# Two attention layers: six mask products become ScalarE copies, batch 0's feed-forward products move into the last body, head 1 comes first

## The chip, the cores and the metric

The kernel runs on one core of a Trainium2 chip. The metric is the device time of one execution in microseconds. A core has five engines with an instruction queue of their own: TensorE (PE, with its weight loads as PEld), VectorE (DVE), ScalarE (ACT), GpSimd (POOL) and SyncE (SP), which here only issues transfers.

## The reference, cut to what matters

Eight batches of 256 tokens with 128 features, fp32, go through two layers; a context of the same shape gives keys and values, with 16 heads of 8 features.

```python
x = x + xattn0(layernorm(x), ctx)          # softmax(q k / sqrt(8)) v, projection; no mask
x = x + ffn(layernorm(x))                  # the feed-forward part
x = x + xattn1(layernorm(x), ctx, mask)    # logits + mask * -1e9, 256 x 256 per batch
x = x + moe(layernorm(x))                  # 8 experts, 512 hidden, the best 2 of a token

def ffn(x):
    h = bit_linear(x, w1)                  # 128 -> 512; rows rounded to 8 bits, weights to -1, 0, 1
    h = silu(depthwise_conv1d(h, conv_w, conv_b))   # 3 taps along the tokens
    return bit_linear(h, w2)               # 512 -> 128; the rows of h rounded to 8 bits
```

## The kernel before, in words

**Order.** Every engine's queue is written out by hand. The program runs in stages: the first layer's attention (35 to 169 us in the profiled execution), its feed-forward part (to 247 us), the second layer's attention (to about 404 us), and the experts, whose tokens are gathered and scattered in DRAM. Semaphores tie the queues; a wait holds everything that stands behind it on its engine.

**Attention as a chain of bodies.** Each engine goes through bodies b = -1, 0, ..., NB (NB = 8), and in a body through the head numbers n = 0 to 15. Body b works on three batches. At head n, for batch b+1, TensorE makes the scores, queries on the partitions (`scores`, L1658), and VectorE takes their row maxima: `plain_max` (L1289) in the first layer, `masked_max` (L1303, one instruction for each half of the keys) in the second. For batch b TensorE makes the same scores again with the keys on the partitions and with the row maximum taken off (`shifted`, L1743), ScalarE takes the exponential of 128 x 512 (L1023), and after every four heads TensorE multiplies with V (`weighted_v`, L1698). For batch b-1 the body finishes: the fourth product with V, `out_transposes` (L1852), VectorE's `head_norm` (L1263, L1269), `norm_transposes` (L1860), ScalarE's copy `o_normT` (L1036), `projection` (L1867), `residual_stats` (L1282, then L428 and L434), GpSimd's `ln_power` (L439, L441), `ln_apply` (L447), and in the first layer `quant_factors` (L458 to L462) and `quantise_rows` on GpSimd. The body NB of the first layer has only finishing work; its second part ("tail") lies inside the first feed-forward steps.

**The mask.** In the second layer a shifted product has three matmuls: first a diagonal matrix times the mask of the batch, 512 columns (L1740), which sets the accumulation to -mask x 1e9, then the two score products with `start=False`.

**How the maxima get into the shifted product.** They are an additional row of the stack `q_stack`. GpSimd's `max_parts` (L817, L819) splits the maxima of eight heads, TensorE transposes them (`max_transposes`, L1635), ScalarE copies them (`maxT`, L967), and a transfer writes them into the stack. Half 0 belongs to the heads 0 to 7, half 1 to the heads 8 to 15. In `extras` the transposes of half 1 stand behind shifted product n = `at["max1"]`.

**Where a step stands.** The table `STEPS` gives for each step the head number of either layer. Keys without a prefix are TensorE's, `a_` is ScalarE's, `d_` VectorE's: `max1` and `a_max1` the transposes and the copy of half 1, `a_out1` the copy of the second half of the output, `d_ln` `ln_apply`, `d_quant` `quant_factors`. `None` means that no head has it.

**PSUM banks.** Scores use banks 0 and 1 in turn, shifted products 2, 3 and 4, the output 5 and 6, and bank 7 the rest. So score n waits for the maximum of head n-2 and a shifted product for the exponential of three heads before (`head_bank`).

**The feed-forward part.** `ffn_hidden` makes the hidden products of a batch in four chunks of 128: half 0 (chunks 0 and 1) with the three taps as three accumulated matmuls (L1674 to L1676), half 1 (chunks 2 and 3) with one matmul each, whose taps then come from ScalarE's `conv_middle` (L915, L916) and VectorE's `conv_sides` (L924, L930). Then `ffn_silu` on ScalarE, `act_transposes` on TensorE (L1954), `quant_scale` on VectorE (the scale of each row), `rounding` on ScalarE (L1155), `quant_clip` on GpSimd (L762, its output f_int), `int_transposes` (L1965), and `output` (L1974). A batch thus passes from engine to engine several times. `ternary_taps` makes the three tap matrices on GpSimd, in body NB-2.

Before the change batch 0's hidden products stand at head 2 of the body NB, behind the wait for the last exponential; batch 1's half 0 at head 8 of the same body, and batch 0's `act_transposes` and batch 1's half 1 behind the body, when the last `head_norm` is done.

Of the kernel before, what the change touches and what calls it, by code (L numbers as in the profile page):

```python
# [18 lines left out]
F32 = mybir.dt.float32  # L19
# [25 lines left out]
    "max1": (0, 2),  # L45
# [12 lines left out]
    "a_out1": (0, 0),  # L58
# [11 lines left out]
    "d_ln": (11, 12),  # L70
# [5 lines left out]
def build(nc, inp, out):  # L76
# [27 lines left out]
    with ExitStack() as ctx:  # L104
# [9 lines left out]
        BANKS_T = (2, 3, 4)  # L114
        BANK_O = (5, 6)
# [185 lines left out]
        class Att:  # L301

            def __init__(self, n):
# [15 lines left out]
                if n == "a0":  # L319
                    return  # L320
                self.k_in, self.k_q, self.k_k = s("mask_in"), s("mask_q"), s("mask_k")
# [442 lines left out]
        def attention_gpsimd(eng, l, part, between={}):  # L764
# [3 lines left out]
            def body(b, r):  # L768
# [55 lines left out]
        def _(eng):  # L824
# [74 lines left out]
            attention_gpsimd(eng, 0, "main 0", {-1: add_output_bias, 0: routing_constants, 1: ternary, NB - 2: ternary_taps})  # L899
# [10 lines left out]
        def conv_middle(eng, b, r):  # L910
# [5 lines left out]
            eng.activation(conv_out[:, r, 1, :], hidden_ps(r, 3), ACT.Copy, scale=conv_w[:, 3, 1:2]).then_inc(h_mid, 1)  # L916

# [94 lines left out]
        def attention_scalar(eng, l, part, between={}):  # L1012
# [305 lines left out]
        def attention_vector(eng, l, part, between={}):  # L1318
# [3 lines left out]
            def body(b, r):  # L1322
                for n in range(H):
# [173 lines left out]

        def ffn_vector(eng):
# [6 lines left out]

            def quant_scale(b):

                for i in range(NT):
                    eng.wait_ge(g_ps, b * NT + i + 1)
# [611 lines left out]
```

## Time and profile before

| | |
|---|---|
| median of 3 runs | 509.7 us (509.5 to 510.54) |
| the profiled execution | 508.18 us, its span 506.4 us |
| TensorE busy | 443.3 us, 88% of the span |
| VectorE busy | 345.9 us, 68% |
| ScalarE busy | 301.6 us, 60% |
| GpSimd busy | 226.5 us, 45% |
| TensorE's mean granted clock | 0.98 of full speed |

The span is from the first to the last instruction that the profiler saw; the execution's time has 1.8 us more around it. The share of an engine is an average over stages with different limits, so the rows below are mostly from single stages. "idle before" in a group of instructions is the time that the engine had nothing to do ahead of them, and the instruction named behind it is the one that ended most of that time.

### The profile page before, as it was taken

The page shows a single profiled execution, that of the slowest core. Times are in us where ns is not written, and L with a number is a line of the kernel's source. Part 1 is how long each engine was busy: PE and PEld are TensorE (multiplying, and loading weights), DVE is VectorE, ACT ScalarE, POOL GpSimd, SP SyncE. Part 2 cuts the span into 40 slices and gives each one's busy share as a digit, 9 for nine tenths or more (in the row PEclk, how much of TensorE's full clock was granted, in tenths as well). Part 3 has the DMA queues.
Part 4 walks back from the last instruction along what each step waited for, and adds up shares of the span by engine and source line. Part 5 has one row for each costly group of instructions (what it writes and reads, how often), then busy time and mean ns, then how long its engine had stood idle before and what let it go on. Part 6 is the DMA issues. An engine that isn't in the chain of part 4 may idle for free.

```text
span 506.4 us, 11481 instructions
## 1 busy us (share of the span) xinstructions
PE 443.3 (88%) x3709; PEld 363.2 (72%) x3709; DVE 345.9 (68%) x1233; ACT 301.6 (60%) x649; POOL 226.5 (45%) x455
## 2 busy tenths in 40 slices
PE   3689999999998779967999999999999889899960
PEld 2477777777775668856778878777777579899960
DVE  6767787878783267877887788787878266444424
ACT  5237776767767448874466756566556555455630
POOL 4752464123216245767200225354453566666650
PEclk9999999999999989989999999999999999999995
DMA  6463323332405995034253234333320301332107
GB/s 216 150 223 105 115 85 116 102 101 77 137 4 207 426 415 213 2 105 130 84 159 113 88 107 158 118 122 94 112 61 2 87 23 39 85 85 82 53 15 249
DMA packets 40698, 61.55 MB, mean 122 GB/s; under 512 B 6121, under 2 KB 30506, under 8 KB 39232
## 3 DMA queue, kind: packets, MB, share of 16 engines
q1 hardware_dynamic: 38080, 56.20, 34.0%
q0 software_dynamic: 2272, 4.24, 2.6%
q8 instruction: 30, 0.49, 0.4%
q10 hardware_dynamic: 288, 0.39, 0.3%
q14 instruction: 28, 0.23, 0.2%
HBM read 31.45 MB, written 29.23 MB: 120 GB/s over the span
## 4 chain that ended last, share of the span: by engine, by line
PE 45%; DVE 10%; issue 5%; ACT 4%; DMA 3%; SPq 2%; POOL 1%; POOLq 0%; DVEq 0%; ACTq 0%
PE ps L1698 6%; PE ps L1658 6%; PE ps L1740 6%; PE ps L1743 5%; PE ps L1889 5%; PE ps L1900 5%; ACT probs L1023 2%; PE ps L1867 1%; DMA k_blocks<-y_dram 1%; DVE ps L1303 1%; PE ps L1954 1%; PE ps L1674 1%; SPq L544 1%; PE ps L1675 1%; PE ps L1676 1%
## 5 line engine op out<-in xcount | busy, mean ns | idle before, releaser
L1023 ACT ACTIVATE probs<-ps 128x512 f32<-128x512 f32 x256 | 147.0, 598 | 79.6 <-PE ps L1743 75.0
L1658 PE MATMUL ps<-k_blocks,q_stacks 128*128 128x256 f32 x512 | 117.9, 314 | 6.4 <-DVE row_max L1289 3.0
L1289 DVE TENSOR_REDUCE row_max<-ps 128x2 f32<-128x512 f32 x144 | 94.9, 686 | 26.9 <-PE ps L1658 25.7
L1743 PE MATMUL ps<-q_stacks,k_blocks 128*128 128x256 f32 x512 | 104.9, 288 | 1.2 <-DMA q_stacks<-maxT 1.0
L1303 DVE CUSTOM_DVE_ANT_0 ps<-ps,mask_q 128x256 f32<-128x256 f32 x224 | 89.8, 452 | 20.6 <-PE ps L1658 18.9
L1743 PEld LDWEIGHTS ps<-q_stacks,k_blocks 128*128 128x128 f32 x512 | 86.8, 189 | 20.8 <-issue 10.6
L1658 PEld LDWEIGHTS ps<-k_blocks,q_stacks 128*128 128x128 f32 x512 | 82.6, 197 | 13.9 <-issue 4.3
L1698 PE MATMUL ps<-probs,v_aug 128*32 128x256 f32 x1024 | 68.5, 385 | 4.3 <-ACT probs L1023 3.1
L817 POOL TENSOR_SCALAR max_split<-row_max 128x16 fp32r<-128x16 f32 x32 | 6.5, 204 | 124.3 <-issue 93.0
L1740 PE MATMUL ps<-mask_k,neg_mask_eye 128*128 128x512 f32 x128 | 54.5, 426 | 0.0
L739 POOL DMA_INDIRECT y_dram<-x_ring x39 | 39.1, 1003 | 22.6 <-ACT x_ring L1102 14.2
L1698 PEld LDWEIGHTS ps<-probs,v_aug 128*32 128x32 f32 x1024 | 27.8, 109 | 24.1 <-ACT probs L1023 6.2
L1889 PE MATMUL ps<-m_xT,m_w 128*128 128x128 f32 x312 | 41.8, 277 | 2.9 <-DVE m_w L1449 1.7
L1900 PE MATMUL ps<-conv_out,m_h 128*128 128x128 f32 x312 | 41.2, 276 | 0.0
L1889 PEld LDWEIGHTS ps<-m_xT,m_w 128*128 128x128 f32 x312 | 37.9, 192 | 4.1 <-DVE m_w L1449 3.0
L1455 DVE COPY conv_out<-experts 128x512 f32 x39 | 18.3, 469 | 31.2 <-PE ps L1900 31.1
L729 POOL DMA_INDIRECT slots_dram<-rows,r_slot x32 | 32.4, 1011 | 13.8 <-issue 7.8
L1900 PEld LDWEIGHTS ps<-conv_out,m_h 128*128 128x128 f32 x312 | 37.9, 192 | 0.0
L1740 PEld LDWEIGHTS ps<-mask_k,neg_mask_eye 128*128 128x128 f32 x128 | 24.0, 188 | 12.8 <-issue 11.9
L1303 DVE DVE_READ_ACCUMULATOR2_ANT row_max<- 128x1 f32 x224 | 31.9, 142 | 0.0
L439 POOL TENSOR_SCALAR ln_ve<-ln_mv 128x2 f32<-128x2 f32 x24 | 5.8, 240 | 52.4 <-DVE ln_mv L434 52.3
L1090 ACT ACTIVATE m_xT<-ps 128x128 f32<-128x128 f32 x39 | 10.8, 277 | 25.1 <-PE ps L1880 25.1
(217 smaller groups left out, 760.1 us busy)
## 6 DMA issues: line engine op xcount, KB each, us to landing
slots_dram<-x_ring SPq DMA_DIRECT2D x1, 10400.0 KB, 30.1
q_stacks<-q_dram SPq DMA_DIRECT2D x32, 256.0 KB
k_blocks<-k_dram SPq DMA_DIRECT2D x128, 48.0 KB
q_dram<-qk_parts SPq DMA_DIRECT2D x16, 256.0 KB, 2.9
k_dram<-qk_parts SPq DMA_DIRECT2D x16, 256.0 KB, 2.9
mask_in<-host_mask SPq DMA_DIRECT2D x8, 512.0 KB, 3.6
experts<-host_experts SPq DMA_DIRECT2D x1, 4096.0 KB, 39.1
x_ring<-slots_dram SPq DMA_DIRECT2D x39, 65.0 KB
```

Source lines behind the costliest of these rows:

```text
L729: eng.indirect_dma_start(out=slots_dram[:, :], out_offset=bass.IndirectOffsetOnAxis(ap=r_slot[r][:, k, i:i + 1], axis=0), in_=rows[:, r, k ...
L739: eng.indirect_dma_start(out=y_dram[:, :], out_offset=bass.IndirectOffsetOnAxis(ap=x_ring[:, slot, D:D + 1].bitcast(U32), axis=0), in_=x_r ...
L1023: eng.activation(probs[:, n // HPS % 2, n % HPS, :, :].rearrange("p k q -> p (k q)"), ps[:, head_bank(BANKS_T, n)[0], :], ACT.Exp).then_in ...
L1289: eng.tensor_reduce(row_max[:, :, n], ps[:, head_bank(BANKS_S, n)[0], :].rearrange("p (i k) -> p i k", i=NT), AX.X, ALU.max).then_inc(a.s_ ...
L1303: last = eng.tensor_tensor_reduce(out=scored, in0=scored, in1=mask_q[t % 2][:, i, :], scale=1.0, scalar=-3.0e38, op0=ALU.add, op1=ALU.max, ...
L1455: eng.tensor_copy(m_down[:, j % 2, :, :].rearrange("p c d -> p (c d)"), experts[:, bass.ds(weight_at[j] + EH, EC * D)]).then_inc(m_weights, 1)
L1658: mm = eng.matmul(ps[:, bank, i * S:(i + 1) * S], q_stack[r][:, st, i * P:(i + 1) * P], k_blocks[r][:, st, j, :], start=not masked, stop=n ...
L1698: mm = eng.matmul(ps[j * HR:(j + 1) * HR, bank, 0:S], v_aug[r][:, k, first:first + HR], probs[:, st % 2, j, k, :], start=(odd == 0 and k = ...
L1740: eng.matmul(ps[:, bank, :], neg_mask_eye[:, :], mask_k[b % 3][:, :, :].rearrange("p i k -> p (i k)"), start=True, stop=False)
L1743: mm = eng.matmul(ps[:, bank, k * S:(k + 1) * S], k_blocks[r][:, st, j, k * P:(k + 1) * P], q_stack[r][:, st, :], start=(l == 0), stop=(l ...
L1889: mm = eng.matmul(ps[:, BANK_W[j % 2], c * P:(c + 1) * P], m_w[:, j % WR, c * P:(c + 1) * P], m_xT[:, j % 2, :], start=True, stop=True)
L1900: mm = eng.matmul(ps[:, BANK_Y[j % 2], 0:D], m_h[:, j % 2, c, :], m_down[:, j % 2, c, :], start=(c == 0), stop=(c == EC - 1))
```

## The change

The parts, by layer:

- First layer: at head 1 of each body TensorE issues score 1, shifted product 1, the transposes of the maxima of half 1 (now `second_max`) and the fourth product with V of the batch before, in this order; until now it was the transposes, score 1, that product with V, and shifted 1. ScalarE's `a_out1` goes from head 0 to head 1.
- First layer: `ln_apply` goes from VectorE to GpSimd, behind `ln_power`.
- `ternary_taps` goes from body 6 to body 3 on GpSimd.
- Batch 0's hidden products go into body 7: half 1 at head 3, chunk 0 at head 6, chunk 1 at head 8. The middle tap of its chunks 2 and 3 is made by VectorE (`first_middle`) at head 6 of that body, the side taps right behind it.
- In the body NB, batch 1's half 1 stands at head 2, its chunk 0 at head 4, and behind `norm_transposes` batch 0's `act_transposes` and batch 1's chunk 1. Batch 0's silu stands at head 2 of ScalarE's body, both halves together; one small silu at the end of body 7 brings its table. VectorE makes batch 0's `quant_scale` at head 6 of the body, and the last batch's `quant_factors` go behind the tail's start.
- Second layer: for the heads 5, 7, 8, 11, 13 and 15 (`SEEDED`) ScalarE copies the mask, times -`MASK_A`, as 128 x 512 numbers from SBUF into the PSUM bank (`mask_seed`), and TensorE leaves out the 512-column product L1740. ScalarE does so behind its exponentials 2, 4, 5, 8, 10 and 12 (`SEED_STEPS`); the copy waits for the end of the exponential that frees the bank.

```diff
@@ STEPS
-    "max1": (0, 2),
+    "max1": (None, 2),
...
-    "a_out1": (0, 0),
+    "a_out1": (1, 0),
...
-    "d_ln": (11, 12),
+    "d_ln": (None, 12),
@@ build
+        SEEDED = (5, 7, 8, 11, 13, 15)
+        SEED_STEPS = (2, 4, 5, 8, 10, 12)
@@ attention_gpsimd, body
                     ln_power(eng, s, b - 1)
+                    if l == 0:
+                        ln_apply(eng, s, b - 1)
...
-            attention_gpsimd(eng, 0, "main 0", {-1: add_output_bias, 0: routing_constants, 1: ternary, NB - 2: ternary_taps})
+            attention_gpsimd(eng, 0, "main 0", {-1: add_output_bias, 0: routing_constants, 1: ternary, 3: ternary_taps})
@@ ScalarE
+        def first_middle(eng):
+
+            eng.wait_ge(h_ps, 1)
+            for c in range(TAPPED, FC):
+                last = eng.tensor_scalar(conv_out[:, 0, c - TAPPED, :], hidden_ps(0, c), conv_w[:, c, 1:2], None, ALU.mult)
+            last.then_inc(h_mid, 1)
...
             if half == 0:
-                eng.wait_ge(h_ps, b * 2 + 1)
+                eng.wait_ge(h_ps, b * 2 + 2)
@@ attention_scalar, body
                                        ps[:, head_bank(BANKS_T, n)[0], :], ACT.Exp).then_inc(a.p_sb, 1)
+                    if l == 1 and exists(b) and n in SEED_STEPS:
+                        mask_seed(b, SEEDED[SEED_STEPS.index(n)])
...
-                    if l == 0 and isinstance(b, int) and b == NB and n == 5:
+                    if l == 0 and b == NB - 1 and n == H - 1:
+                        eng.activation(r_gap[:, :], minus_half[:, 0:NT], ACT.Silu)
+                    if l == 0 and b == NB and n == 2:
                         eng.wait_ge(a.pv, NB * 4 - 1)
-                        conv_middle(eng, 0, 0)
                         ffn_silu(eng, 0, 0, 0)
-                    if l == 0 and isinstance(b, int) and b == NB and n == 10:
                         ffn_silu(eng, 0, 0, 1)
...
+            def mask_seed(b, n):
+
+                if n == SEEDED[0]:
+                    eng.wait_ge(a.k_k, b + 1)
+                eng.wait_ge(a.p_sb, b * 16 + n - 2 if n < H - 1 else b * 16 + 12)
+                eng.activation(ps[:, head_bank(BANKS_T, n)[0], :],
+                               mask_k[b % 3][:, :, :].bitcast(F32).rearrange("p i k -> p (i k)"),
+                               ACT.Copy, scale=-MASK_A).then_inc(a.t_seed, 1)
@@ attention_vector, body
-                    if n == at["d_ln"] and exists(b - 1):
-                        if l == 0:
-                            ln_apply(eng, s, b - 1)
-                        else:
-                            ln_rows(eng, b - 1, 1 - r)
-                    if l == 0 and n == at["d_quant"] and exists(b - 1):
+                    if l == 1 and n == at["d_ln"] and exists(b - 1):
+                        ln_rows(eng, b - 1, 1 - r)
+                    if l == 0 and n == at["d_quant"] and exists(b - 1) and b < NB:
                         quant_factors(eng, s, b - 1)
-                    if l == 0 and isinstance(b, int) and b == NB and n == 6:
+                    if l == 0 and n == 0 and b == NB + 1:
+                        quant_factors(eng, s, NB - 1)
+                    if l == 0 and b == NB - 1 and n == 6:
+                        first_middle(eng)
                         conv_sides(eng, 0, 0)
+                    if l == 0 and b == NB and n == 6:
+                        quant_scale(eng, 0)
@@ ffn_vector, step (quant_scale itself is moved out of it, unchanged)
-                quant_scale(b)
+                if b > 0:
+                    quant_scale(eng, b)
@@ attention_tensor, body
+                    ahead = l == 0 and n == at["pv"] % HPS and exists(b)
+                    if ahead:
+                        shifted(b, r, n)
+                        second_max(b)
                     if n % HPS == at["pv"] % HPS:
...
-                    if exists(b):
+                    if exists(b) and not ahead:
                         shifted(b, r, n)
                     extras(b, r, n)
+
+            def second_max(b):
+
+                if after(b, 0):
+                    eng.wait_ge(a.o_sb, b * 2 - 1)
+                max_transposes(eng, l, b, 1)
@@ shifted
-                if l == 1:
+                seeded = l == 1 and n in SEEDED
+                if seeded:
+                    eng.wait_ge(a.t_seed, b * len(SEEDED) + SEEDED.index(n) + 1)
+                elif l == 1:
                     eng.matmul(ps[:, bank, :], neg_mask_eye[:, :], mask_k[b % 3][:, :, :].rearrange("p i k -> p (i k)"),
                                start=True, stop=False)
...
-                                    q_stack[r][:, st, :], start=(l == 0), stop=(l == 0 or k == NT - 1))
+                                    q_stack[r][:, st, :], start=(l == 0), stop=(l == 0 or k == NT - 1),
+                                    skip_group_check=seeded)
@@ extras (ffn_hidden takes a tuple of chunks now)
-                if l == 0 and isinstance(b, int) and b == NB and n == 2:
+                if l == 0 and b == NB - 1 and n == 3:
 
                     eng.wait_ge(a.s_max, NB * 16)
+                    eng.wait_ge(f_tern, 9)
+                    ffn_hidden(eng, 0, 0, 1)
+                if l == 0 and b == NB - 1 and n in (6, 8):
+                    ffn_hidden(eng, 0, 0, 0, (n // 2 - 3,))
+                if l == 0 and b == NB and n == 2:
                     eng.wait_ge(a.p_sb, NB * 16)
-                    eng.wait_ge(f_tern, 9)
-                    for half in range(2):
-                        ffn_hidden(eng, 0, 0, half)
-                if l == 0 and isinstance(b, int) and b == NB and n == 8:
-                    ffn_hidden(eng, 1, 1, 0)
+                    ffn_hidden(eng, 1, 1, 1)
+                if l == 0 and b == NB and n == 4:
+                    ffn_hidden(eng, 1, 1, 0, (0,))
...
                 if n == at["max1"] and exists(b):
-                    if after(b, 0):
-                        eng.wait_ge(a.o_sb, b * 2 - 1)
-                    max_transposes(eng, l, b, 1)
+                    second_max(b)
...
                         norm_transposes(eng, l, b - 1)
+                        if l == 0 and b == NB:
+                            act_transposes(eng, 0)
+                            ffn_hidden(eng, 1, 1, 0, (1,))
@@ ffn_tensor (act_transposes itself is moved out of it, unchanged)
-
-            eng.wait_ge(att[0].o_norm, NB * 2)
-            act_transposes(0)
-            ffn_hidden(eng, 1, 1, 1)
```

## Rows read from the trace of the kernel before

**Rows 1.** The page: busy us of each engine, share of the span, instructions.

```profile
PE 443.3 (88%) x3709; PEld 363.2 (72%) x3709; DVE 345.9 (68%) x1233; ACT 301.6 (60%) x649; POOL 226.5 (45%) x455
```

**Rows 2.** Windows: stretch, length, busy PE PEld DVE ACT POOL (count), granted clock, DMA, GB/s.

```profile
35.50:153.50 118.00, 111.49 (x1058) 86.69 (x1058) 94.96 (x219) 85.01 (x169) 38.24 (x80) 1.00 0.31 93
169.40:193.90 24.50, 20.40 (x114) 17.64 (x111) 12.56 (x39) 13.53 (x30) 7.18 (x13) 0.93 1.03 428
264.10:387.00 122.90, 122.31 (x1055) 96.22 (x1055) 101.18 (x511) 75.66 (x162) 48.14 (x141) 1.00 0.34 104
```

**Rows 3.** Groups by line and form: busy, mean ns of one | idle before them.

```profile
L967 ACT ACTIVATE maxT<-ps 8x512 f32<-8x512 f32 x32 | 18.5, 579 | 8.9 <-PE ps L1635 8.4
...
L1222 ACT ACTIVATE k_blocks<-o_normT 128x2048 fp32r<-128x2048 f32 x2 | 3.8, 1916 | 0.0
...
L447 POOL TENSOR_SCALAR xn<-x_res,ln_mv,ln_rstd 128x128 f32<-128x128 f32 x16 | 12.7, 798 | 0.9
...
L447 DVE TENSOR_SCALAR xn<-x_res,ln_mv,ln_rstd 128x128 f32<-128x128 f32 x16 | 4.8, 344 | 3.1 <-POOL ln_rstd L441 2.5
```

**Rows 4.** Timeline, start of body 4: start, us, instruction, count [wait before it].

```profile
101.67 0.40 PE L1743 MATMUL ps<-q_stacks,k_blocks 128*128 128x256 f32 x2
...
102.65 0.41 PE L1635 MATMUL ps<-ident_r,max_split 128*8 128x128 f32 x4 [0.58 <-POOL max_split L819]
...
104.62 0.40 PE L1658 MATMUL ps<-k_blocks,q_stacks 128*128 128x256 f32 x2
```

**Rows 5.** Timeline, end of body 4.

```profile
115.33 0.60 DVE L447 TENSOR_SCALAR xn<-x_res,ln_mv,ln_rstd 128x128 f32<-128x128 f32 x2
...
117.05 0.41 DVE L458 TENSOR_REDUCE qa<-xn 128x2 f32<-128x256 f32 x1
...
118.60 0.47 PE L1658 MATMUL ps<-k_blocks,q_stacks 128*128 128x256 f32 x2 [0.30 <-DVE row_max L1289]
```

**Rows 6.** Timeline, body 7 and the start of the feed-forward part.

```profile
157.91 1.07 PE L1698 MATMUL ps<-probs,v_aug 128*32 128x256 f32 x16 [0.48 <-ACT probs L1023]
...
160.87 0.71 PE L1867 MATMUL ps<-w_all,o_normT 128*128 128x128 f32 x4 [0.20 <-ACT o_normT L1036]
...
165.23 1.07 PE L1698 MATMUL ps<-probs,v_aug 128*32 128x256 f32 x16 [1.03 <-ACT probs L1023]
...
169.40 0.70 PE L1674 MATMUL ps<-xnT_all,w_taps 128*128 128x256 f32 x2
...
172.95 0.60 PE L1852 MATMUL ps<-ident,o_raw 128*128 128x128 f32 x4
...
177.27 0.61 PE L1867 MATMUL ps<-w_all,o_normT 128*128 128x128 f32 x4
...
186.76 1.30 POOL L762 TENSOR_SCALAR f_int<-probs 128x512 bf16<-128x512 int16 x2
...
188.59 1.06 PE L1965 MATMUL ps<-ident_bf,f_int 128*128 128x128 bf16 x8
```

**Rows 7.** Waits of TensorE's weight loads, 264 to 388 us: total us, times, longest.

```profile
PEld ps L1867 <- ACT o_normT L1036: 1.4, 6, 0.2
...
PEld ps L1658 <- DVE row_max L1303: 1.0, 4, 0.3
```

**Rows 8.** Timeline, a full body of the second layer.

```profile
331.19 0.60 PE L1852 MATMUL ps<-ident,o_raw 128*128 128x128 f32 x4
...
335.79 0.30 PEld L1658 LDWEIGHTS ps<-k_blocks,q_stacks 128*128 128x128 f32 x2 [0.26 <-DVE row_max L1303]
...
345.65 0.40 PE L1740 MATMUL ps<-mask_k,neg_mask_eye 128*128 128x512 f32 x1
345.89 0.40 PE L1743 MATMUL ps<-q_stacks,k_blocks 128*128 128x256 f32 x2
...
352.07 0.60 PE L1852 MATMUL ps<-ident,o_raw 128*128 128x128 f32 x4
```

**Rows 9.** Timeline, last body of the second layer.

```profile
401.13 1.07 PE L1698 MATMUL ps<-probs,v_aug 128*32 128x256 f32 x16 [0.38 <-ACT probs L1023]
```

More of the change, by code:

```diff
@@ L320, in __init__ @@
                     return
+                self.t_seed = s("t_seed")
                 self.k_in, self.k_q, self.k_k = s("mask_in"), s("mask_q"), s("mask_k")
@@ L1496, in moe_vector, with quant_scale @@
                 eng.tensor_tensor(part, part, y_back[:, g, 1, :], ALU.add).then_inc(y_added, 1)
+        def quant_scale(eng, b):
+            for i in range(NT):
+                eng.wait_ge(g_ps, b * NT + i + 1)
+                last = eng.tensor_reduce(fa[:, 0, i:i + 1], ps[:, 4 + i, :], AX.X, ALU.max, apply_absolute_value=True)
+                last.then_inc(g_stat, 1)
+            eng.wait_ge(g_stat, b * 5 + 2)
+            if after(b, 0):
+                eng.wait_ge(g_round, b * NT)
+            eng.tensor_scalar(fa[:, 3, :], fa[:, 0, :], QUANT_EPS, 1.0 / 127.0, ALU.max, ALU.mult).then_inc(g_stat, 1)
+            eng.wait_ge(g_stat, b * 5 + 3)
+            if after(b, 0):
+                eng.wait_ge(fa_kept, b)
+            eng.reciprocal(fa[:, 1, :], fa[:, 3, :]).then_inc(g_stat, 1)
+            eng.tensor_scalar(fa[:, 2, :], fa[:, 3, :], wq_stat[:, 3:4], None, ALU.mult).then_inc(g_stat, 1)
         def ffn_vector(eng):
@@ L1504, in keep_factors @@
                 eng.tensor_copy(fa_last[:, :], fa[:, 2, :]).then_inc(fa_kept, 1)
-            def quant_scale(b):
-                for i in range(NT):
-                    eng.wait_ge(g_ps, b * NT + i + 1)
-                    last = eng.tensor_reduce(fa[:, 0, i:i + 1], ps[:, 4 + i, :], AX.X, ALU.max, apply_absolute_value=True)
-                    last.then_inc(g_stat, 1)
-                eng.wait_ge(g_stat, b * 5 + 2)
-                if after(b, 0):
-                    eng.wait_ge(g_round, b * NT)
-                eng.tensor_scalar(fa[:, 3, :], fa[:, 0, :], QUANT_EPS, 1.0 / 127.0, ALU.max, ALU.mult).then_inc(g_stat, 1)
-                eng.wait_ge(g_stat, b * 5 + 3)
-                if after(b, 0):
-                    eng.wait_ge(fa_kept, b)
-                eng.reciprocal(fa[:, 1, :], fa[:, 3, :]).then_inc(g_stat, 1)
-                eng.tensor_scalar(fa[:, 2, :], fa[:, 3, :], wq_stat[:, 3:4], None, ALU.mult).then_inc(g_stat, 1)
             def residual(b):
@@ L1546, in ffn_vector @@
             keep_factors(NB - 2)
-            quant_scale(NB - 1)
+            quant_scale(eng, NB - 1)
             low_parts(eng, 1, 1, BANKS_HEAD[1])
@@ L1660, in scores, with ffn_hidden @@
             mm.then_inc(a.s_ps, 1)
-        def ffn_hidden(eng, b, r, half):
+        def ffn_hidden(eng, b, r, half, chunks=None):
             if after(b, 1):
@@ L1667, in ffn_hidden @@
             x = one(xnT_all, b)
-            for c in range(2 * half, 2 * half + 2):
+            for c in chunks or range(2 * half, 2 * half + 2):
                 h = hidden_ps(r, c)
@@ L1721, in body @@
                             weighted_v(eng, l, b, r, (n - at["pv"]) // HPS)
-                    if exists(b):
+                    if exists(b) and not ahead:
                         shifted(b, r, n)
                     extras(b, r, n)
+            def second_max(b):
+                if after(b, 0):
+                    eng.wait_ge(a.o_sb, b * 2 - 1)
+                max_transposes(eng, l, b, 1)
             def shifted(b, r, n):
@@ L1946, in moe_tensor, with act_transposes @@
                 step(j)
-        def ffn_tensor(eng):
-            def act_transposes(b):
-                eng.wait_ge(h_act, 2 * (b + 1))
-                for i in range(NT):
-                    eng.wait_ge(g_round, b * NT)
-                    for c in range(FC):
-                        mm = eng.transpose(ps[:, 4 + i, c * P:(c + 1) * P], f_act[:, c, i * P:(i + 1) * P], ident[:, :])
-                    mm.then_inc(g_ps, 1)
+        def act_transposes(eng, b):
+            eng.wait_ge(h_act, 2 * (b + 1))
+            for i in range(NT):
+                eng.wait_ge(g_round, b * NT)
+                for c in range(FC):
+                    mm = eng.transpose(ps[:, 4 + i, c * P:(c + 1) * P], f_act[:, c, i * P:(i + 1) * P], ident[:, :])
+                mm.then_inc(g_ps, 1)
+        def ffn_tensor(eng):
             def int_transposes(b):
@@ L2011, in ffn_tensor @@
             tokens(NB - 5)
-            act_transposes(NB - 2)
+            act_transposes(eng, NB - 2)
             int_transposes(NB - 3)
@@ L2016, in ffn_tensor @@
             tokens(NB - 4)
-            act_transposes(NB - 1)
+            act_transposes(eng, NB - 1)
             eng.wait_ge(ln_f0.xs, 2)
```

3 lines of the change are left out of this document (1 added, 2 removed).

## The prediction, made before the changed kernel had run

> **What bounds the kernel now.** I read the busy shares first, then the stages, then the waits inside them. Over the whole span TensorE is busy 88%, VectorE 68% and ScalarE 60% [rows 1]. By stage, the second layer's full bodies are the purest TensorE stretch: 122.31 of 122.90 us busy, against 101.18 for VectorE and 75.66 for ScalarE [rows 2]. In the first layer TensorE has 6.5 us of 118 free, and around the start of the feed-forward part (169.4 to 193.9 us) 4.1 of 24.5. So a matmul that leaves TensorE's queue in the second layer shortens it, unless another engine's turn comes at once. Whether it does is seen in who TensorE waits for there: four times VectorE's row maxima held a score by up to 0.3 us, and six times ScalarE's output copy held the projection by 0.2 us [rows 7]. Two other chains thus lie close behind TensorE in a few places of each body.
>
> **The change, part by part.** The first layer's bodies 0 to 6 take 118 us, 17 each [rows 2]; a full body of the second layer takes 20.9 (331.19 to 352.07 [rows 8]).
>
> *Head 1 opens the bodies (first layer).* Now shifted 0 starts at 101.67, and the transposes of the row maxima stand behind it and wait until 102.65 for GpSimd's split; score 1, a product with V and shifted 1 follow, and score 2 starts at 104.62 [rows 4]. A head's two matmuls take 0.24 us from start to start (345.65 to 345.89 is the mask product, of the same 512 columns [rows 8]), so shifted 0 has left TensorE by 101.91. New: score 1 and shifted 1 (0.47) are issued inside this wait, up to 102.38, and the transposes still start at 102.65. What stood behind them is shorter by 0.47, so score 2 starts at about 104.1: 0.5 saved. Bodies 2 to 6 show this wait in full, body 1 half of it, body 0 none, and body 7 has no scores to put there. I take 5 x 0.5 + 0.3 + 0.2 = 3.0 us; bounds 1.5 (VectorE's maxima give half back) and 3.5.
>
> *Rows on GpSimd.* The two applications take 0.60 us on VectorE from 115.33 [rows 5]; on GpSimd 2 x 0.80 = 1.60 [rows 3], so they end at 116.95 instead of 115.93. But VectorE uses the result only at 117.05, since two maxima stand between [rows 5]. These now run during GpSimd's turn, the factors start at 117.0 to 117.1 as before, and so the maximum that frees score 0 at 118.60 ends as before. Cost and gain are both about 0, with hardly any cover: whatever GpSimd takes beyond 1.60 is paid in every body. The ternary taps, moved to an earlier body, lie in GpSimd's long wait between the two splits of a body (GpSimd is busy 38 of 118 us [rows 2]) and hold nobody.
>
> The row shows 16 applications on GpSimd, all in the feed-forward part beside a working VectorE, at a mean of 798 ns [rows 3]. The Trainium skill (GPSIMD Engine Reference, Key points) says that GpSimd shares its SBUF interfaces with VectorE and contends with it when VectorE is in a two-port mode or reads two SBUF inputs. By the row the sum stands; by the rule the step may be longer. What that would do is rival C, worked out from rows.
>
> *Batch 0's products in the last body.* They take 3.5 us (169.40 to 172.95 [rows 6]) and go to heads 3, 6 and 8 of body 7. TensorE waits in that body, but the long waits, 1.03 at 165.23 and a like one before the last product with V, come behind head 8. What lies before, 0.48 at 157.91 and 0.20 at 160.87 [rows 6] and half a us between these, is about 1.2. So the last product with V ends 2.3 us later. Behind it TensorE needs 7.87 now to the projection (169.40 to 177.27 [rows 6]): batch 0's 3.5, transposes, a wait for the normalisation, and batch 1's taps, 2.6. New it is batch 1's middle (0.9), output transposes (0.5), one tap chunk (1.3), normalised transposes (0.3), activation transposes (1.0) and the other chunk (1.3): 5.3. That is 2.6 less against 2.3 more, so the projection comes 0.3 earlier. Silu's table is loaded under the last product with V. From the projection on, the chain is statistics, power, application (1.0 longer, by the step above), factors, rounding, masks, and GpSimd's f_int(0). It began at 186.76 and now begins 0.7 later; but TensorE took it only at 188.59, 0.5 after its end (186.76 + 1.30 [rows 6]), because batch 1's activation transposes stood ahead, and these are now long done. Net 0. Bounds: 0.8 won if body 7 hides 2 us, 1.5 lost if it hides none and the products behind the longer idle time run at the lower clock (the granted clock of this stretch is 0.93 now [rows 2]).
>
> *Six mask copies (second layer).* Each takes one 512-column product out of TensorE's order, 0.24 us from start to start [rows 8]: 1.42 a body. ScalarE copies 128x512 from SBUF to PSUM instead. No row shows such a copy; the nearest are 579 ns for 512 columns out of PSUM and 1916 ns for 2048 within SBUF, a quarter of which is 479 [rows 3]. I take 0.6, nearest to the row of the same width; bounds 0.48 and 0.7. The copy waits for the end of ScalarE's own exponential. Six times 0.65 is 3.9 us on the 12.9 that ScalarE is busy in a body (75.66 / 122.9 x 20.9): 16.8, still below TensorE.
> What remains of the 1.42 depends on what is late next. In a full body the output transposes are issued at 331.19; from there VectorE works without a break (normalisation, maximum 4, router, low parts, maximum 5) and frees score 7 only at 335.79, for which TensorE waited 0.26 [rows 8]: head 5 saves nothing. Head 7 brings its exponential and with it the output's copy and the projection 0.24 forward; head 8 stands ahead of that same wait [rows 7]: nothing. From score 9 to score 12 VectorE's chain of residual and statistics is the pace: head 11 nothing. Heads 13 and 15 are TensorE's own, less 0.1 for the maximum that frees the next body's score 0. So 0.6 a body, for six bodies 3.6. The first body lacks these chains: 1.42 less 0.3 is 1.1. In the last body ScalarE is the pace: its product with V waited 0.38 for head 11's exponential [rows 9], and now the copy for head 13 stands before that exponential (0.65 to 0.8 more), while 0.34 is won once behind it: 0.4 lost. Together 3.6 + 1.1 - 0.4 = 4.3 us. Bounds: 0.4 lost if VectorE holds everything, 11.4 won (48 x 0.237) if every product counts.
>
> **Sum.** 3.0 + 0 + 0 + 4.3 = 7.3 us off. The profiled execution took 508.18 us (its span 506.4) and would take 500.9; the median of the runs shown, 509.7, lies 1.5 above it and becomes 502.4 us.
>
> **Rivals.**
> *A, VectorE already bounds the second layer.* For it: the waits for maxima [rows 7] and 101.18 busy of 122.9 [rows 2]. Against it: TensorE is busy in 99.5% of the stretch, and after heads 13 and 15 nothing holds it by more than 0.1. The copies give nothing and cost the last body's 0.4: 509.7 - 3.0 + 0.4 = 507.1.
> *B, every mask product counts.* For it: the same 99.5%. Against it: the same waits. 509.7 - 3.0 - 11.4 = 495.3.
> *C, slower: GpSimd's application becomes the first layer's pace.* What it takes beyond 1.60 us is paid in six bodies and once before the feed-forward part. At twice the duration, 3.2 us, that is 7 x 1.6 = 11.2: 509.7 - 7.3 + 11.2 = 513.6. It decides from 7.3 / 7 = 1.04 us more each. Against it: 16 rows with a mean of 798 ns [rows 3]. This is what the skill's rule cited above would do here.
>
> **Chances and range.** The case of the sum has 0.62, with 499.5 to 505.5 of its own. A 0.15, B 0.08, C 0.06; 0.09 is left for mixtures, of which some half end near no change or above it. The range 498 to 507.5 takes in A and leaves B and C out. Faster by over 0.2% (1 us, about what a measurement of this kernel can tell from no change) 0.87, within it 0.05, slower 0.08.
>
> **What would show it.** Bodies 2 to 6 take 16.7 instead of 17.2 us, and the transposes of the maxima wait at most 0.3. The factors' reduction starts as far behind the power as now; if it comes 1 us later, C. f_int(0) ends 0.5 to 1 us later after body 7's start than now, with its transposes right behind it. There are 48 copies into PSUM of about 0.6; full bodies of the second layer take 20.3, the first 1.1 less, the last 0.4 more. Longer waits for maxima at scores 7 and 12 with bodies of 20.9 are A's sign, bodies of 19.5 are B's. The prediction is wrong if the copies last 0.9 or more, if they delay exponentials in full bodies as in the last one, or if the idle time ahead of f_int(0) keeps TensorE's clock low for longer than now.

## The result

The changed kernel takes 508.31 us (median of 20 runs, 506.18 to 510.63), the kernel before 509.72 us on the same chip (20 runs). The ratio is 0.9966, interval 0.995 to 0.9981: faster by 0.34% (1.7 us by the ratio, 1.4 by the two medians). Forecast were 502.4 us and 1.4%. That is outside the range of 498 to 507.5 us, and slower than rival A's 507.1.

The page of the changed kernel, its share of busy time:

```profile
PE 439.5 (87%) x3661; PEld 357.2 (71%) x3661; DVE 340.9 (67%) x1219; ACT 324.9 (64%) x696; POOL 239.9 (47%) x471
```

TensorE is 3.8 us less busy than in [rows 1] and ScalarE 23 us more, yet the profiled span is 506.2 us, where it was 506.4. Windows of the changed kernel, columns as in [rows 2]: first-layer bodies, start of the feed-forward part, a part of it by itself, the second layer's full bodies, and 7.4 us behind the last body.

```profile
35.70:152.70 117.00, 113.83 (x1060) 88.77 (x1059) 92.02 (x207) 84.83 (x169) 49.75 (x95) 0.98 0.31 93
169.70:193.30 23.60, 18.35 (x110) 14.76 (x111) 9.85 (x33) 12.61 (x29) 10.19 (x17) 0.86 1.04 429
183.50:190.75 7.25, 4.38 (x17) 3.22 (x18) 1.75 (x4) 4.32 (x10) 4.40 (x8) 0.53 1.08 446
264.60:384.40 119.80, 116.88 (x1024) 89.94 (x1022) 100.83 (x512) 94.28 (x199) 48.06 (x141) 1.00 0.35 108
405.30:412.70 7.40, 6.50 (x31) 6.04 (x32) 3.19 (x17) 3.07 (x10) 3.96 (x11) 0.54 0.08 27
```

The number ahead of the last two is the granted clock. It shows stretches of 7 us at the lower level (0.5, that is 1.2 GHz), around 184 and 406 us, and the 0.98 of the first row comes from one around 36 us. The first profile of the kernel before had half as long a one (3.4 us) at the start of the feed-forward part, the 0.93 of [rows 2], and none at the other two places.

The stages of three profiled executions in us, each body from its first exponential to the next body's, the last one to the end of its last exponential. The middle column is a second profile of the unchanged kernel (an experiment below):

| | before, first profile | before, second profile | changed |
|---|---|---|---|
| up to body 0's first exponential | 35.9 | 36.2 | 36.1 |
| body 0 | 14.5 | 15.7 | 16.2 |
| bodies 1 to 6 | 103.1 | 103.1 | 100.4 |
| body 7 and feed-forward part | 93.5 | 92.3 | 94.2 |
| second layer, first body | 17.5 | 17.5 | 17.7 |
| second layer, six bodies | 123.2 | 123.1 | 119.8 |
| second layer, last body | 16.7 | 16.6 | 17.3 |
| behind it | 102.0 | 104.2 | 104.3 |

The two large gains (2.7 and 3.3 us) are there, and with 20.4 us for a full body of the second layer neither A (20.9) nor B (19.5) came. The rest of the table gives much of them back.

**Head 1's order.** The start of body 4 in the changed kernel's timeline:

```profile
102.36 0.48 PE L1684 MATMUL ps<-k_blocks,q_stacks 128*128 128x256 f32 x2
102.67 0.40 PE L1782 MATMUL ps<-q_stacks,k_blocks 128*128 128x256 f32 x2
103.05 0.40 PE L1661 MATMUL ps<-ident_r,max_split 128*8 128x128 f32 x4
103.38 1.07 PE L1724 MATMUL ps<-probs,v_aug 128*32 128x256 f32 x16
104.38 0.51 PE L1684 MATMUL ps<-k_blocks,q_stacks 128*128 128x256 f32 x2
```

The maxima's transposes wait no more (0.58 in [rows 4]). Score 2 comes 1.88 us behind the body's first exponential (102.50) instead of 2.51 (102.11). The body is 16.81 instead of 17.24 us.

**GpSimd's application**, from the end of the same body and from the groups by line:

```profile
115.38 1.60 POOL L450 TENSOR_SCALAR xn<-x_res,ln_mv,ln_rstd 128x128 f32<-128x128 f32 x2
117.01 0.42 DVE L461 TENSOR_REDUCE qa<-xn 128x2 f32<-128x256 f32 x1 [0.44 <-POOL xn L450]
```
```profile
L450 POOL TENSOR_SCALAR xn<-x_res,ln_mv,ln_rstd 128x128 f32<-128x128 f32 x32 | 25.5, 801 | 1.8
```

32 applications at 801 ns, where [rows 3] had 16 at 798: two take 1.60 us, and VectorE now waits 0.44 for them. The body is as long as with the application on VectorE (an experiment below). The Trainium skill (GPSIMD Engine Reference, Key points) warns of contention between the two engines; here the application takes no longer in the bodies than in [rows 3], but VectorE works beside it there too, and no run has it alone.

**The copies** take 598 ns each:

```profile
L1094 ACT ACTIVATE ps<-mask_k 128x512 f32<-128x512 f32 x48 | 28.7, 598 | 1.7
```

A full second-layer body takes 20.4 us (20.9 before). The first one did not gain. Some of its waits (total us, times, longest):

```profile
PE ps L1684 <- DVE row_max L1326: 0.8, 2, 0.5
DVE qk_parts L1336 <- ACT qk_parts L1066: 0.6, 1, 0.6
```

VectorE's low parts wait 0.6 for ScalarE's high parts, and scores wait 0.8 for maxima, for which none waited in this body of the kernel before. I first read this as one chain: the copy for head 5 pushes exponential 3 and the high parts behind it back, and the maxima come later.

**The last body.** TensorE's rows, the last product with V behind which heads 13 to 15 stand, and the transposes of the rows:

```profile
398.71 1.07 PE L1724 MATMUL ps<-probs,v_aug 128*32 128x256 f32 x16 [1.17 <-ACT probs L1035]
...
403.86 0.41 PE L1888 MATMUL ps<-ident,rows 128*128 128x128 f32 x2 [2.93 <-DVE rows L1384]
```

The wait for ScalarE is 1.17 instead of 0.38 [rows 9]. TensorE then waits 2.93 us for VectorE's rows, instead of 1.95.

**The start of the feed-forward part**, changed kernel:

```profile
169.67 1.07 PE L1724 MATMUL ps<-probs,v_aug 128*32 128x256 f32 x16 [1.19 <-ACT probs L1035]
...
175.75 0.61 PE L1911 MATMUL ps<-w_all,o_normT 128*128 128x128 f32 x4
...
184.93 0.66 PE L483 MATMUL ps<-ident,xn 128*128 128x128 f32 x2 [3.24 <-POOL xn L477]
186.94 1.30 PE L2009 MATMUL ps<-ident_bf,f_int 128*128 128x128 bf16 x8 [1.35 <-POOL f_int L765]
188.03 1.16 PE L1700 MATMUL ps<-xnT_all,w_taps 128*128 128x256 f32 x2
...
193.31 1.04 PE L1997 MATMUL ps<-ident,probs 128*128 128x128 f32 x8
```

TensorE has done its products by 181.7 and waits 3.24 and 1.35 us for GpSimd. The clock falls at 183.9 (window 183.50:190.75 above), and the products that follow take twice their time: from the int transposes (186.94) to batch 2's activation transposes (193.31) 6.4 us. In the second profile of the kernel before, where the clock stayed up, it is 5.0:

```profile
189.20 0.66 PE L1965 MATMUL ps<-ident_bf,f_int 128*128 128x128 bf16 x8
189.69 0.65 PE L1674 MATMUL ps<-xnT_all,w_taps 128*128 128x256 f32 x2
...
194.21 1.09 PE L1954 MATMUL ps<-ident,probs 128*128 128x128 f32 x8 [0.41 <-ACT probs L944]
```

### The profile page after: what moved, and what is told of

Its sections match the earlier page's. It is cut to its first block, busy times and chain, and to the rows that moved or that the text cites. A ratio compares the mean times of both kernels' runs of the same rounds, so it can differ in the third digit from the quotient of the medians.

```text
span 506.2 us, 11482 instructions
## 1 busy us (share of the span) xinstructions
PE 439.5 (87%) x3661; PEld 357.2 (71%) x3661; DVE 340.9 (67%) x1219; ACT 324.9 (64%) x696; POOL 239.9 (47%) x471
## 4 chain that ended last, share of the span: by engine, by line
PE 39%; DVE 13%; ACT 6%; issue 6%; POOL 3%; DMA 2%; DVEq 0%; POOLq 0%; SPq 0%; ACTq 0%
PE ps L1933 7%; PE ps L1944 5%; PE ps L1684 5%; PE ps L1724 4%; PE ps L1782 4%; DVE ps L1326 3%; ACT probs L1035 3%; PE ps L1779 2%; PE ps L1911 1%; DMA k_blocks<-y_dram 1%; DVE ln_st L431 1%; PE ps L1997 1%; PE ps L1700 1%; PE ps L1701 1%; PE ps L1702 1%
## 5 line engine op out<-in xcount | busy, mean ns | idle before, releaser
L1782 PE MATMUL ps<-q_stacks,k_blocks 128*128 128x256 f32 x512 | 107.0, 293 | 1.4 <-DMA q_stacks<-maxT 0.8
L1326 DVE CUSTOM_DVE_ANT_0 ps<-ps,mask_q 128x256 f32<-128x256 f32 x224 | 89.5, 451 | 17.6 <-PE ps L1684 15.7
L1782 PEld LDWEIGHTS ps<-q_stacks,k_blocks 128*128 128x128 f32 x512 | 84.3, 191 | 23.2 <-issue 9.7
L1933 PE MATMUL ps<-m_xT,m_w 128*128 128x128 f32 x312 | 43.5, 284 | 2.8 <-DVE m_w L1474 1.6
L1933 PEld LDWEIGHTS ps<-m_xT,m_w 128*128 128x128 f32 x312 | 39.6, 199 | 3.6 <-DVE m_w L1474 2.9
L1779 PE MATMUL ps<-mask_k,neg_mask_eye 128*128 128x512 f32 x80 | 33.8, 422 | 0.0
L1094 ACT ACTIVATE ps<-mask_k 128x512 f32<-128x512 f32 x48 | 28.7, 598 | 1.7
```

Of the source, the lines that this page charges most:

```text
L1094: eng.activation(ps[:, head_bank(BANKS_T, n)[0], :], mask_k[b % 3][:, :, :].bitcast(F32).rearrange("p i k -> p (i k)"), ACT.Copy, scale=-M ...
L1326: last = eng.tensor_tensor_reduce(out=scored, in0=scored, in1=mask_q[t % 2][:, i, :], scale=1.0, scalar=-3.0e38, op0=ALU.add, op1=ALU.max, ...
L1779: eng.matmul(ps[:, bank, :], neg_mask_eye[:, :], mask_k[b % 3][:, :, :].rearrange("p i k -> p (i k)"), start=True, stop=False)
L1782: mm = eng.matmul(ps[:, bank, k * S:(k + 1) * S], k_blocks[r][:, st, j, k * P:(k + 1) * P], q_stack[r][:, st, :], start=(l == 0), stop=(l ...
L1933: mm = eng.matmul(ps[:, BANK_W[j % 2], c * P:(c + 1) * P], m_w[:, j % WR, c * P:(c + 1) * P], m_xT[:, j % 2, :], start=True, stop=True)
```

## The experiments

Runs of one group shared a chip; the kernel before took 510.53 us (22 runs) beside the first four, 510.26 (29 runs) beside the next four, 510.09 (20 runs) beside the last four.

**First group: the copies and the stretch behind the last body.** The copies' heads become a function of the batch. Each of three runs has one of these lines:

```diff
+        def seeds_of(b):
+            return ()                                                           # no copies
+            return SEEDED if b < NB - 1 else ()                                 # none in the last body
+            return () if b == NB - 1 else (13, 15) if b == 0 else SEEDED        # trimmed
```

> The changed kernel without any of the six mask copies; all else of the change stays. Theory K (the copies win about 3.1 us in the second layer's bodies and give all of it back in its last body and behind it, where TensorE's longer idle time is followed by a stretch at the lower clock): same time as the changed kernel, about 508.3 us, 1.4 to 2 below before; full bodies back at 20.9 us, last body 16.8, granted clock 1.00 between 405 and 425 us. Rival S (the copies win on the whole, and the changed kernel would stand at 511 without them): 510 to 511.5 us. Rival L (the copies cost on the whole, through the work they put on ScalarE): under 507 us.

Measured: 509.22 us, ratio 0.998 (0.9958 to 1.0001). Full bodies take 20.9 us as expected, the last one 16.4 instead of the 16.8 expected and the 16.7 of the kernel before. But the clock fell behind the last body all the same:

```profile
408.00:416.00 8.00, 7.63 (x50) 7.38 (x49) 3.27 (x21) 2.53 (x9) 2.47 (x8) 0.72 0.06 20
```

So theory K falls in the link that mattered to it: the copies do not make that stretch. The time lies between K's and S's. Against the kernel before this run wins 1.3 us by the medians, the changed kernel 1.4 (1.0 and 1.7 by the ratios): timed as a whole, the six copies in all eight bodies are worth 0.1 to 0.7 us, on two chips.

> The changed kernel, but the last body of the second layer makes all its mask products on TensorE as before; the other seven bodies keep the six copies. Theory K: the last body is back at 16.8 us, the half-clock stretch behind it is gone, and 0.7 + 2.4 us come back: 505.2 us. Rival R (the half-clock stretch at 405 us came with something else, so it stays): only the body's 0.7, 507.6 us.

Measured: 506.68 us, 0.9918 (0.9889 to 0.9947). The last body is back at 16.4 us and the stretch stays (it is at 403.7 to 410.5 us here), so R's mechanism held. The time does not decide: as it stands it is nearer R's 507.6, by the ratio (505.5 us beside a kernel before of 509.72) nearer K's 505.2. Beside the run without copies 2.5 us are won: the copies are worth having in the full bodies.

```diff
@@ extras, ahead of the rows' transposes of the last body
+                        for _ in range(9):
+                            eng.matmul(ps[:, BANKS_S[0], :], neg_mask_eye[:, :],
+                                       mask_k[b % 3][:, :, :].rearrange("p i k -> p (i k)"), start=True, stop=True)
```

> The changed kernel with all its copies; behind the last shifted product TensorE issues nine products of the mask's form (512 columns, some 0.24 us each, 2.1 us) into a bank that nobody reads, in the 2.9 us in which it waits for the rows. They compute nothing that is used. Theory K: the rows' transposes come at the same time, but the clock stays at the full level behind them and the 2.35 us that the stretch to 412.9 us lost come back: 506.0 us. Rival R: the half-clock stretch stays and the time is 508.3 us or a little more.

Measured: 505.79 us, 0.9906 (0.987 to 0.9941), as K said. Between 400 and 416 us the clock is 1.00 throughout, and the part behind the last body takes 102.6 us instead of 104.3. The stretch goes when the idle time ahead of it is filled. All three profiles with this wait filled lack it (the later ones are below), and one of the eleven with it unfilled does, the first of the kernel before: the idle time allows the fall and does not force it.

> As the run without copies in the last body, and the first body of the second layer (batch 0) keeps only the copies for heads 13 and 15. Theory K with its reading of the first body (the copies for heads 5, 7 and 8 push exponential 3 and the high parts back by 0.55 us, and VectorE's low parts wait for them): the first body falls from 17.7 to 17.2 us, and the time from 505.2 to 504.7 us. Rival: the body's loss comes with the copies 11 to 15, and nothing changes against that run.

Measured: 506.61 us, 0.9928 (0.99 to 0.9955), no other time than the run before it. The first body takes 17.73 us, with all six copies 17.74, and without any (the first run of this group) 17.85. In the run without copies one score of this body still waits for a maximum:

```profile
PE ps L1691 <- DVE row_max L1333: 0.4, 1, 0.4
```

So the copies for heads 5 to 11 harm it as little as they help, and my reading of its chain falls. Its lengths in the later runs go with another part, the start of the feed-forward part. With copies it takes 17.7 to 17.8 us where that start is wholly the new one, 17.39 with the application back on VectorE, 17.48 with batch 0's products back, 17.35 to 17.39 with the whole old start, and 17.5 in the kernel before. What the new start changes there stays open.

**Second group: the kernel before once more, a filled wait in it, and single undo runs.**

> The kernel before, unchanged, for a second profile of it. The run without any copies also showed TensorE at the lower clock from 405.2 to 412.6 us, so the copies don't make that stretch. Theory N (it comes in most executions of the kernel before too, and its first profile is one without it): granted clock about 0.973 and a stretch at half clock near 405 us, 101.9 us behind the last exponential become 103.5 to 104. Rival K (only the changed kernel and its relatives have it): granted clock 0.981 again and none.

Measured: 510.36 us, clock 0.972. Two windows of it, around the start of the feed-forward part and behind the last body:

```profile
180.00:193.00 13.00, 10.32 (x62) 9.05 (x63) 9.19 (x28) 7.99 (x19) 6.08 (x12) 1.00 1.06 427
```
```profile
408.00:416.00 8.00, 7.31 (x49) 7.09 (x50) 4.05 (x22) 2.94 (x12) 3.48 (x9) 0.79 0.08 27
```

Theory N holds: the first profile of the kernel before, from which I forecast, was one with a high clock behind the last body (the 29 clocks of this kernel beside this run lie between 0.959 and 0.984, most at 0.970 to 0.976; that profile had 0.981), and one with a stretch at 187.1 to 190.5 us that this one lacks.

> The kernel before with the nine unused 512-column products in TensorE's wait for the rows of the second layer's last body (its wait was 1.95 us, so they push the transposes back by up to 0.2). Theory N: the stretch at half clock is usual in the kernel before and goes away: about 508.3 us against 510.5 on this chip's earlier runs, 0.4% less. Rival K: no stretch to take away, so the same time as before or 0.2 us more.

Measured: 508.81 us, 0.9965 (0.9944 to 0.9987): 1.4 us less, N again. The nine products stand ahead of the rows, and the clock stays at 1.00:

```profile
404.38 2.27 PE L1805 MATMUL ps<-mask_k,neg_mask_eye 128*128 128x512 f32 x9
406.49 0.38 PE L1847 MATMUL ps<-ident,rows 128*128 128x128 f32 x2
```
```profile
408.00:416.00 8.00, 6.98 (x60) 6.46 (x60) 4.96 (x24) 4.30 (x15) 4.81 (x13) 1.00 0.09 27
```

```diff
@@ STEPS
-    "d_ln": (None, 12),
+    "d_ln": (11, 12),
@@ attention_gpsimd
-                    if l == 0:
-                        ln_apply(eng, s, b - 1)
@@ attention_vector
-                    if l == 1 and n == at["d_ln"] and exists(b - 1):
-                        ln_rows(eng, b - 1, 1 - r)
+                    if n == at["d_ln"] and exists(b - 1):
+                        if l == 0:
+                            ln_apply(eng, s, b - 1)
+                        else:
+                            ln_rows(eng, b - 1, 1 - r)
```

> The changed kernel with the first layer's application of the normalisation back on VectorE at head 11. Theory G (the move to GpSimd is free in the bodies and costs its own 1.0 us once, in the chain ahead of the feed-forward part): bodies 2 to 6 stay at 16.8 us, f_int(0) comes 1.0 us earlier, time 507.3 us, 0.2% below the changed kernel. Rival V (the shorter bodies come from VectorE's relief, not from head 1's order): bodies 2 to 6 rise to 17.0 to 17.2 us and the time to 509.5.

Measured: 508.80 us, 0.9973 (0.995 to 0.9996). Bodies 2, 4 and 5 stay at 16.8 and body 6 at 16.6 us (body 3 takes 17.2): G holds there, V falls. The 1.0 us was not won. Behind the last application VectorE has batch 1's taps ahead of the factors:

```profile
177.97 0.60 DVE L450 TENSOR_SCALAR xn<-x_res,ln_mv,ln_rstd 128x128 f32<-128x128 f32 x2 [1.27 <-POOL ln_rstd L444]
178.49 0.87 DVE L934 SCALAR_TENSOR_TENSOR conv_out<-ps,conv,conv_out 128x255 f32<-128x255 f32 x2
179.39 0.88 DVE L940 SCALAR_TENSOR_TENSOR conv_out<-ps,conv,conv_out 128x255 f32<-128x255 f32 x2
180.18 0.41 DVE L461 TENSOR_REDUCE qa<-xn 128x2 f32<-128x256 f32 x1
```

The factors come 28.6 us behind body 7's first exponential, 0.5 later than behind GpSimd's application.

> The changed kernel with batch 0's feed-forward products, taps and silu, and batch 1's, back at their old places (the old body NB). Theory H (the move shifts work by the same amount, as the prediction's sum had it, and what it wins in TensorE's order is lost to the stretch at half clock at 184 to 191 us): body 7 falls from 16.9 to 14.9 us, what is between its last exponential and the second layer's first rises from 77.3 to 79.3, and the time stays within 0.5 us of the changed kernel's. Rival M (the move costs 1 us or more through that stretch): 507.3 us or less. Rival W (it wins on the whole): 509.3 us or more.

Measured: 509.71 us, 0.999 (0.9974 to 1.0007), against 0.9966 (0.995 to 0.9981) for the changed kernel: no better, which seems to speak for W. But the run kept the last factors behind the tail's start, where they now stood behind batch 0's scale and batch 1's taps: they began 30.4 us behind body 7's first exponential, instead of 27.7 in the kernel before. It shows that this place puts the factors off by 2.7 us, not what the move wins. Hence the next run.

**Third group: whole undo, a filled wait, one part alone, all together.** The next kernel is the changed one with the three undo edits together (application, batch 0, factors at head 13); only the ternary taps stay in body 3.

> The changed kernel with the whole start of the feed-forward part as it was: batch 0's and batch 1's products, taps and silu at their old places, the application on VectorE and the last factors at head 13. Head 1's order and the six copies stay. The two undo runs before this one took back only one of these each and left VectorE's queue in a mixed order. Theory F (the new start costs about 2 us: TensorE is done early, waits 3.2 and 1.35 us for GpSimd, and works at half clock to 190.7 us, while the old start keeps it busy up to the int transposes): from body 7's start to the second layer's first exponential 92.2 us instead of 94.2, no stretch at half clock near 185 us in this profile, time 506.3 us. Rival Q (the new start is worth what the old one is, and the differences seen are the clock's chance): 508.0 to 508.5 us.

Measured: 506.14 us, 0.9923 (0.9897 to 0.9949). From body 7's first exponential to the second layer's 92.35 us; int transposes at 34.3 and batch 2's activation transposes at 39.3, as in the second profile of before. Theory F holds: the new start costs about 2 us (2.2 by the medians and by the ratios, on two chips).

```diff
+        def keep_busy(eng, bank, times):
+            for _ in range(times):
+                eng.matmul(ps[:, bank, S:2 * S], w1[:, 2, :], one(xnT_all, 0), start=True, stop=True)
@@ attention_tensor, ahead of xn_transposes
+                    if b == NB + 1:
+                        keep_busy(eng, BANK_M, 6)
@@ int_transposes
+                if b == 0:
+                    keep_busy(eng, 6, 2)
```

> The changed kernel; TensorE issues six unused products of 256 columns (0.43 us each by the hidden products' rows) in its 3.2 us wait ahead of the last batch's row transposes, and two in its 1.35 us wait ahead of the first int transposes. Nobody reads them. Theory F: the int transposes start 34.2 us behind body 7's first exponential as now, but at full clock, and batch 2's activation transposes come 5.0 instead of 6.4 us later; 94.2 us of that part become 92.8 and the time 506.8 us. Rival D (the lost time is in the longer chain over GpSimd, not in the clock): 508.3 us or more.

Measured: 504.71 us, 0.9893 (0.9862 to 0.9925), more than F said. The timeline and the clock of the stretch:

```profile
179.90 2.75 PE L1996 MATMUL ps<-xnT_all,ffn_w 128*128 128x256 f32 x12
183.22 0.44 PE L483 MATMUL ps<-ident,xn 128*128 128x128 f32 x2 [0.57 <-POOL xn L477]
...
186.25 0.65 PE L1700 MATMUL ps<-xnT_all,w_taps 128*128 128x256 f32 x2
...
190.19 1.04 PE L2003 MATMUL ps<-ident,probs 128*128 128x128 f32 x8
```
```profile
180.00:193.00 13.00, 11.34 (x74) 9.40 (x73) 5.85 (x19) 7.44 (x17) 6.93 (x13) 1.00 1.00 414
```

The chain over GpSimd is as long as before (f_int at 33.5 us behind body 7's start in both), TensorE's work behind it is 1.5 us shorter, and D falls for the most part. The part takes 92.9 us, 1.3 less than in the changed kernel's profile and still 0.6 more than the old start at full clock; why was not tried. By the times the filling won 3.6 us on two chips, and no stage shows the other 2.3: this profile also lacks the stretch around 36 us (body 0 takes 14.3 instead of 16.2), which I take for chance.

> The kernel before with head 1's order alone (score 1, shifted 1 and the maxima's transposes ahead of the product with V; the output's second copy at head 1). Theory O: it alone makes the shorter bodies, 16.8 instead of 17.2 us in bodies 2 to 6 and 0.3 less in body 1: 2.7 us, time 507.6 us. Rival V (it needs VectorE's relief as well): bodies at 17.0 to 17.2 us, time 509.5.

Measured: 507.70 us, 0.9955 (0.9932 to 0.9979). Bodies 2 to 6 are 16.8, 17.2, 16.8, 17.0 and 16.4 us. Theory O: head 1's order does it alone, VectorE's relief adds 0.35 us in one body of six (body 3, 17.2 against 16.8).

> Head 1's order and the old start of the feed-forward part; the six copies in the second layer's full bodies, two (heads 13 and 15) in its first and none in its last; the nine unused products in the last wait for the rows. If the parts add up: 510.3 - 2.7 (order) - 3.3 (copies in seven bodies) - 1.5 to 2.1 (the stretch at half clock behind the last body) = 502.5 us, 1.5% below the kernel before. Rival (the clock takes its stretch elsewhere once it is kept up here): 504.5 us.

Measured: 502.19 us (499.82 to 505.52, 6 runs), 0.9838 (0.9802 to 0.9873), 1.6% below the kernel before. The parts add up to within the noise. Its profile still has the chance stretches near 35 and 188 us.

## Why the prediction was wrong

The direction and the mechanisms of the two main gains were right, and the size of the whole was not: 7.3 us forecast, 1.4 to 1.7 measured. From the second profile of the kernel before to the changed one the span falls by 2.4. Of the 4.9 us short of 7.3, 1.8 are at the start of the feed-forward part, 2.1 in the copies, 0.4 in head 1's order, and most of the rest is the clock around 36 us.

- *Head 1's order, 3.0 us.* Right: 2.6 to 2.7 between the profiles, 2.4 (510.09 less 507.70) when timed alone.
- *Rows on GpSimd, 0.* Right in the bodies, duration and cover as said; rival C did not come.
- *Batch 0's products in the last body, "Net 0".* **This step failed.** The chain was sized well: the last product with V 2.1 us later (2.3 forecast), f_int(0) 0.3 later (0.7), and TensorE takes it at once. What I kept only as a bound, products "at the lower clock", is the normal case: a TensorE that is done early waits 3.24 us and starts at half clock. The six profiles with the new start and its wait unfilled (the changed kernel and five experiments) all have a stretch there, of 7 to 10 us, and 94.2 to 95.5 us for the part. Of the six with the old start two have one, of 3.4 us, and 93.5 and 93.9 us; the other four have none, and 92.0 to 92.4. So the step costs 1.8 us against the second profile, more than my bound of 1.5, and only 0.6 against the first, from which I forecast: that one had a stretch here itself. Undone, it brings back 2.2 us; with the wait filled, 1.3 of the 1.8 go.
- *The copies, 4.3 us.* Full bodies: 3.4 us against the first profile, 3.2 against the second, 3.6 forecast; the duration of a copy was right too. The first body: 1.1 forecast, 0.1 measured (17.85 without copies, 17.74 with them). This term failed as well. In the kernel before no score of that body waits for maxima, so it does lack this chain; but VectorE is close enough behind that with the copies scores wait 0.8 in two places, where without them one waits 0.4. The last body: 0.4 forecast as a loss, 0.7 measured, and 0.9 against the same kernel without copies (17.3 against 16.4). This term counted the copy for head 13 alone: those for heads 5, 7 and 8 had already put exponential 8 off by 0.5 us (9.07 us behind the body's first one, without copies 8.56). The product with V that waits stands 1.1 us later, and 0.2 are won behind it.
- *The offset.* The sum was made against one execution, which had 0.981 as its mean clock, and 1.5 us were added for the distance to the median as if that were constant. The second profile is 2.2 us longer than the first, and its stretches account for that: one at 36 us adds 1.2 to body 0, one at 408 us adds 2.3 behind the last body, and the lack of one at 187 us takes 1.2 off. Of the 14 profiles 8 have the one at 36, and of the 11 with an unfilled last wait 10 have the one behind the last body: the base was the exception.

With the second profile as base the stages account for the difference: -2.6 (bodies 1 to 6), +1.8 (feed-forward start), +0.3, -3.2 and +0.7 (second layer), +0.1 (behind it), +0.5 (start, clock): -2.4 us, against a ratio whose interval reaches from -1.0 to -2.5 us. The profiles with and without the copies put them at 2.4 us (3.2 + 0.1 - 0.9) and the times at 0.1 to 0.7; which holds stays open. So does what of the remaining distance to the median is chance of the clock, and what is a stretch that the changed kernel has more often. The granted clocks (0.951 to 0.967, against mostly 0.970 to 0.976 before) speak for the second.

## What to carry to other kernels

Where TensorE is the bound, work taken from it is worth its duration only if the idle time that it leaves does not drop the clock of what follows: look for the waits ahead of dense work (here 1.9 to 3.2 us), and price what stands right behind them at up to twice its time (a pair of 256-column products took 1.16 instead of 0.65 us). Before a single profile becomes the base of a sum, hold its mean granted clock against those of the other executions. Of the 71 executions of the kernel before that ran beside the experiments, two had more than 0.976, both 0.984, and were the fastest, 507.1 and 507.2 us. It is a warning and no measure: four with 0.962 or 0.963 took only 508.2 to 508.6. An undo run must restore the queue order of every engine that the part touched, else it measures a third order that neither kernel has.

## What the runs showed of the hardware

Nine or eight matmuls that nobody reads, put into a wait, made the kernel faster by 1.4 us (kernel before, last wait) and 3.6 us (changed kernel, feed-forward start, two chips; 1.5 expected, and 1.3 seen in the stage). The fall need not follow one long wait, and the same waits need not bring it: in the second profile of the kernel before, TensorE waited 1.94 and 0.64 us and was busy in 7.31 of the 8 us from 408 on, and these ran at a mean clock of 0.79; in the first profile the same queue with the same waits (1.95 and 0.64) stayed at 1.00. The Trainium skill (TensorE: Matmul & The Clock Gate, Part 1) says that the monitor of TensorE's activity runs free of the kernel, so that the point of a change differs from run to run; that two profiles of one kernel differ in this way agrees with it.
